# Banded attention scores and value products on quarters of TensorE's array, inside an attention and mixture-of-experts block

## The reference

```python
HEADS, HEAD_DIM, RADIUS = 16, 16, 7            # WIN = 15 keys around each query
qkv = xn @ qkv_w + qkv_b
scores = einsum('bld,blwd->blw', q, kw) / sqrt(HEAD_DIM)   # kw: the 15 keys around each token, zero padded
attn = softmax(scores, axis=-1)
out = einsum('blw,blwd->bld', attn, vw)                    # vw: the same window of the values
out = out @ proj_w + proj_b
```

## Time and profile before

| what | value |
|---|---|
| time, median of 3 runs | 2010.96 us (2010.38 to 2011.26) |
| time of the profiled execution | 2008.52 us |
| span of its instructions | 2006.8 us |
| PE busy in the span | 1978.0 us, 99% |
| PE weight loads busy | 1811.9 us, 90% |
| DVE busy | 1469.7 us, 73% |
| ACT busy | 1135.3 us, 57% |
| POOL busy | 923.8 us, 46% |
| granted TensorE clock, mean | 0.999 |

### The profile page before, as it was taken

One profiled execution on the slowest core, in us unless ns is written; L12 is line 12 of the kernel. 1 busy time (PEld: TensorE's weight loads), 2 busy tenths in 40 slices (PEclk: granted clock), 3 DMA queues, 4 the chain that ended last, 5 costly groups with the idle time before them and its releaser, 6 DMA issues.

```text
span 2006.8 us, 37534 instructions
## 1 busy us (share of the span) xinstructions
PE 1978.0 (99%) x13454; PEld 1811.9 (90%) x13454; DVE 1469.7 (73%) x2462; ACT 1135.3 (57%) x1801; POOL 923.8 (46%) x909
## 2 busy tenths in 40 slices
PE   7899999999999999999999999999999999999999
PEld 6789999999999999999999999999999999999998
DVE  8686786867868687786877868678686877868743
ACT  5465555646556555565655566465565555655554
POOL 6336254363434635255271553625446353453635
PEclk9999999999999999999999999999999999999999
DMA  4121211212112121121211102121021211212111
GB/s 122 32 64 53 54 53 32 70 49 69 49 32 64 43 74 44 48 58 32 74 53 53 48 27 74 53 61 52 29 72 43 74 43 46 55 38 74 43 58 53
DMA packets 188848, 108.79 MB, mean 54 GB/s; under 512 B 65436, under 2 KB 187640, under 8 KB 188664
## 3 DMA queue, kind: packets, MB, share of 16 engines
q1 hardware_dynamic: 187316, 105.43, 18.5%
q10 hardware_dynamic: 1348, 0.98, 0.2%
HBM read 85.52 MB, written 8.39 MB: 47 GB/s over the span
## 4 chain that ended last, share of the span: by engine, by line
PE 89%; DVE 6%; ACT 2%; issue 2%; SPq 0%; POOL 0%; DMA 0%; ACTq 0%; DVEq 0%; POOLq 0%
PE psB L233 48%; PE psA L233 25%; PE psA L1095 5%; PE psA L1122 5%; PE psA L1107 3%; PE psA L1010 2%; DVE pr L631 1%; DVE smax L627 1%; DVE hr_lo L553 1%; DVE qm L596 1%; DVE acc L569 1%; ACT hr_hi L860 0%; ACT pr L909 0%; ACT L909 0%; DVE rinv L629 0%
## 5 line engine op out<-in xcount | busy, mean ns | idle before, releaser
L553 DVE TENSOR_TENSOR hr_lo<-hf,hr_hi 128x512 fp32r<-128x512 f32 x512 | 485.7, 949 | 432.6 <-ACT hr_hi L860 431.9
L860 ACT ACTIVATE hr_hi<-hf 128x512 fp32r<-128x512 f32 x512 | 323.7, 632 | 272.8 <-PE psB L233 184.7
L440 POOL TENSOR_TENSOR wx_lo<-raw,wx_hi 128x512 fp32r<-128x512 f32 x256 | 393.4, 1537 | 21.4
L438 POOL TENSOR_SCALAR wx_hi<-raw 128x512 fp32r<-128x512 f32 x256 | 191.2, 747 | 363.6 <-PE psB L233 349.5
L856 ACT ACTIVATE hf<-psB,b1x 128x512 f32<-128x512 f32 x256 | 175.1, 684 | 199.4 <-PE psB L233 197.7
L233 PE MATMUL psB<-wx_hi,hr_hi 128*128 128x256 f32 x1024 | 287.5, 281 | 0.2
L233 PE MATMUL psB<-wx_hi,hr_lo 128*128 128x256 f32 x1024 | 286.3, 280 | 0.0
L233 PE MATMUL psB<-wx_lo,hr_hi 128*128 128x256 f32 x1024 | 285.7, 279 | 0.0
L454 POOL TENSOR_SCALAR kb<-kT 64x384 f32<-64x384 f32 x128 | 78.5, 613 | 351.3 <-ACT kT L876 343.4
L233 PE MATMUL psB<-z_hi,wx_hi 128*128 128x512 f32 x512 | 210.8, 412 | 0.0
L233 PE MATMUL psB<-z_hi,wx_lo 128*128 128x512 f32 x512 | 202.3, 395 | 0.0
(11 more groups left out here) (153 smaller groups left out, 5121.8 us busy)
## 6 DMA issues: line engine op xcount, KB each, us to landing
raw<-in_L_ffn_W1e SPq DMA_DIRECT2D x256, 128.0 KB, 2.2
raw<-in_L_ffn_W2e SPq DMA_DIRECT2D x256, 128.0 KB, 2.1
out_x<-acc SPq DMA_DIRECT2D x32, 256.0 KB, 2.2
xin<-in_L_attn_x SPq DMA_DIRECT2D x15, 512.0 KB, 3.8
vb<-vs SPq DMA_DIRECT2D x64, 96.0 KB
vb<-vs SPq DMA_DIRECT2D x62, 80.0 KB
tm<-in_L_ffn_b2e SPq DMA_DIRECT2D x32, 128.0 KB, 3.0
raw<-in_L_attn_fc_w SPq DMA_DIRECT2D x8, 256.0 KB, 4.0
```

What stands on the lines that cost most here:

```text
L438: g.tensor_scalar(wx[0][:, s, :], raw[:, s, :], 1.0, 0.0, ALU.mult, ALU.add).then_inc(w_hi.sem, 1)
L440: g.tensor_tensor(wx[1][:, s, :], raw[:, s, :], wx[0][:, s, :].bitcast(f32), ALU.subtract).then_inc(w_lo.sem, 1)
L553: v.tensor_tensor(hr[1][:, c % 2, :], hf[:, c % 3, :], hr[0][:, c % 2, :].bitcast(f32), ALU.subtract).then_inc(h_lo.sem, 1)
L860: a.activation(hr[0][:, c % 2, :], hf[:, c % 3, :], ACT.Copy).then_inc(h_hi.sem, 1)
```

## The change

1. **Scores** (scores): each block is now four products in place of one. Product (gr, n) takes features 64gr to 64gr+63 (a group of four heads) and two of the four copies of the queries: 64 rows by 64 columns of qm loaded, 64 by 48 of kT moving. The result goes to partitions 64n to 64n+63 of bank gr. All eight blocks of a unit fill both banks, 48 columns each, so one semaphore increment for each unit stands where there were two.
2. **No kb.** The windows are read in kT itself. POOL's copies (8 a row) go, and with them the semaphore kb; ACT's next write of kT, and DVE's of qm, now wait for score.
3. **Softmax layout.** pr is 128 by 16 by 64, of which 48 are used and 16 stay zero from a memset. mask h now reads bank h, which holds all blocks of one group, and writes with a gap.
4. **Transposes** have 112 columns in place of 96, and ACT's copies 112 partitions.
5. **attend**: each block is four products: 48 keys by 32 features (two heads) of vb loaded, 48 by 64 of pT (the same two heads) moving; the result goes to partitions 64gr + 32n of bank 2 + gr. vb has 64 features a row in place of 128 half empty.
6. **attended**: four operations as before, each on 64 partitions by 256, with emask (two heads) in place of hmask. POOL makes emask at the start, nine short operations more.

The core of the diff:

```diff
-    PK = G * KW
+    GW = 64
+    PK = GW + KW
+    HP = 32
...
-        kb = sb("kb", [P, 2, UB, G * KW])
...
-        vb = sb("vb", [PK, HS, NT, KD, P])
-        pr = sb("pr", [P, 2, UB, G, KW])
+        vb = sb("vb", [PK, HS, NT, KD, GW])
+        pr = sb("pr", [P, 2, UB, G, GW])
...
             def mask(t, u):
                 for h in range(2):
-                    v.wait_ge(score.sem, score.at(t, 2 * u + h))
+                    v.wait_ge(score.sem, score.at(t, u))
...
-                        pr[:, u % 2, 4 * h:4 * h + 4, :, :].rearrange("p b g k -> p (b g) k"),
-                        psA[:, h, 0:4 * G * KW].rearrange("p (n k) -> p n k", k=KW), HD ** -0.5,
-                        band[:, :].unsqueeze(1).to_broadcast([P, 4 * G, KW]), ALU.mult, ALU.add).then_inc(masked.sem, 1)
+                        pr[:, u % 2, :, h, 0:KW], psA[:, h, 0:UB * KW].rearrange("p (b k) -> p b k", k=KW), HD ** -0.5,
+                        band[:, :].unsqueeze(1).to_broadcast([P, UB, KW]), ALU.mult, ALU.add).then_inc(masked.sem, 1)
...
-                src = psA[:, 2:4, :].rearrange("p h (b s q) -> p (h b) s q", s=HS, q=QB)
-                dst = aT[:, c, th * UB * QB:(th + 1) * UB * QB].rearrange("p (b q) -> p b q", q=QB)
-                for s in range(HS):
-                    if s:
-                        v.wait_ge(aT_s.sem, aT_s.at(t, HS * u + s - 1))
-                        v.scalar_tensor_tensor(dst, src[:, :, s, :], hmask[:, s:s + 1], dst, ALU.mult, ALU.add).then_inc(aT_s.sem, 1)
-                    else:
-                        v.tensor_scalar(dst, src[:, :, s, :], hmask[:, s:s + 1], None, ALU.mult).then_inc(aT_s.sem, 1)
+                for n in range(2):
+                    for gr in range(G):
+                        rows = slice(GW * gr, GW * gr + GW)
+                        src = psA[rows, 2 + gr, :].rearrange("p (b n q) -> p b n q", n=2, q=QB)[:, :, n, :]
+                        dst = aT[rows, c, th * UB * QB:(th + 1) * UB * QB].rearrange("p (b q) -> p b q", q=QB)
+                        if n:
+                            v.wait_ge(aT_s.sem, aT_s.at(t, HS * u + gr))
+                            v.scalar_tensor_tensor(dst, src, emask[rows, n:n + 1], dst, ALU.mult, ALU.add).then_inc(aT_s.sem, 1)
+                        else:
+                            v.tensor_scalar(dst, src, emask[rows, n:n + 1], None, ALU.mult).then_inc(aT_s.sem, 1)
...
             def keys(t, c):
...
-                    a.wait_ge(kb_s.sem, kb_s.at(t, 3))
+                    a.wait_ge(score.sem, score.at(t, 1))
                 elif t:
-                    a.wait_ge(kb_s.sem, kb_s.all(t - 1))
+                    a.wait_ge(score.sem, score.all(t - 1))
...
             def scores(t, u):
...
-                    for j in range(4):
-                        b = 4 * h + j
-                        last = pe.matmul(psA[:, h, j * PK:(j + 1) * PK], qm[:, th, b, :], kb[:, th, b, :], start=True, stop=True)
-                    last.then_inc(score.sem, 1)
+                for b in range(UB):
+                    at = (th * UB + b) * QB
+                    for gr in range(G):
+                        rows = slice(GW * gr, GW * gr + GW)
+                        for n in range(2):
+                            cols = slice(2 * QB * n, 2 * QB * n + 2 * QB)
+                            last = pe.matmul(psA[cols, gr, b * KW:(b + 1) * KW], qm[rows, th, b, cols], kT[rows, at:at + KW], start=True, stop=True)
+                last.then_inc(score.sem, 1)
...
             def attend(t, u):
...
                     for j in range(4):
-                        last = pe.matmul(psA[:, 2 + h, j * P:(j + 1) * P], vb[:, j, 2 * th + h, c, :], pT[0:PK, 4 * h + j, :], start=True, stop=True)
+                        b = 4 * h + j
+                        for gr in range(G):
+                            keys = slice(GW * gr, GW * gr + KW)
+                            for n in range(2):
+                                to, cols = GW * gr + HP * n, slice(2 * QB * n, 2 * QB * n + 2 * QB)
+                                last = pe.matmul(psA[to:to + HP, 2 + gr, 2 * QB * b:2 * QB * (b + 1)], vb[keys, j, 2 * th + h, c, HP * n:HP * n + HP],
+                                                 pT[keys, b, cols], start=True, stop=True)
                     last.then_inc(av.sem, 1)
```

More of the change, by code:

```diff
@@ L109, in build @@
         hmask = sb("hmask", [P, HS])
+        emask = sb("emask", [P, 2])
         nb = sb("nb", [P, NT])
@@ L212, in build @@
         tr1, t1_f0, t1_f1, t1_hi, t1_lo = signal("tr1", KD), signal("t1_f0"), signal("t1_f1"), signal("t1_hi", KD), signal("t1_lo", KD)
[L213 removed]
+        qk, kT_s, qm_even, qm_odd = signal("qk", 4), signal("kT", KD), signal("qm_even", 8), signal("qm_odd", 8)
         val, vs_s, vb_in = signal("val", 2), signal("vs", 2), signal("vb_in", 12, 16)
[L215 removed]
+        score, masked, smax_s, shifted = signal("score", 4), signal("masked", 8), signal("smax", 4), signal("shifted", 4)
         exped, ssum, rinv_s = signal("exped", 4), signal("ssum", 4), signal("rinv", 4)
@@ L265, in windows @@
                 for gr in range(G):
-                    dst = vb[KW * gr + key:KW * gr + key + n, s, tiles[0]:tiles[-1] + 1, :, 64 * gr:64 * gr + 64]
+                    dst = vb[GW * gr + key:GW * gr + key + n, s, tiles[0]:tiles[-1] + 1, :, :]
                     src = vs[at:at + n, tiles[0] - back:tiles[-1] + 1 - back, :].rearrange("p i (c g n) -> p i c g n", c=KD, g=G)[:, :, :, gr, :]
@@ L407, in _ @@
             roots(1, *EXTRA[1])
[L408 to L412, removed]
+            for m, n in ((hmask, HS), (emask, 2)):
+                const(g.memset(m[:, :], 1.0))
+                for h in range(0, P, HD * n):
+                    v = m[h:h + HD * n, :]
+                    const(g.affine_select(out=v, in_=v, compare_op=ALU.is_ge, fill=0.0, base=0, pattern=[[-HD, n]], channel_multiplier=1))
+                    const(g.affine_select(out=v, in_=v, compare_op=ALU.is_ge, fill=0.0, base=HD - 1, pattern=[[HD, n]], channel_multiplier=-1))
             const(g.memset(band[:, :], 0.0))
@@ L440, in split @@
                 g.tensor_tensor(wx[1][:, s, :], raw[:, s, :], wx[0][:, s, :].bitcast(f32), ALU.subtract).then_inc(w_lo.sem, 1)
[L442 to L456, removed]
             def norm1_bias(t):
@@ L481, in _ @@
                         continue
[L482 to L487, removed]
+                    if q == 2 and t == 0:
+                        weights(8, 10)
+                        norm1_bias(0)
+                        weights(10, 13)
                     elif q == 7 and t:
@@ L590, in query_blocks @@
                 if c:
-                    v.wait_ge(score.sem, score.at(t, 2 * (u - 2) + 1))
+                    v.wait_ge(score.sem, score.at(t, u - 2))
                 elif t:
-                    v.wait_ge(score.sem, score.at(t - 1, 2 * (u + 2) + 1))
+                    v.wait_ge(score.sem, score.at(t - 1, u + 2))
                 src = psA[:, 3 if c or t == 0 else 1, th * UB * QB:(th + 1) * UB * QB].rearrange("p (b q) -> p b q", q=QB)
@@ L881, in query_blocks @@
                 if c:
-                    a.wait_ge(score.sem, score.at(t, 2 * (u - 2) + 1))
+                    a.wait_ge(score.sem, score.at(t, u - 2))
                 elif t:
-                    a.wait_ge(score.sem, score.at(t - 1, 2 * (u + 2) + 1))
+                    a.wait_ge(score.sem, score.at(t - 1, u + 2))
                 src = psA[:, 3 if c or t == 0 else 1, th * UB * QB:(th + 1) * UB * QB].rearrange("p (b q) -> p b q", q=QB)
@@ L899, in query_blocks_first @@
                 a.wait_ge(qk.sem, qk.at(t, 1))
-                a.wait_ge(score.sem, score.at(t - 1, 5))
+                a.wait_ge(score.sem, score.at(t - 1, 2))
                 src = psA[:, 1, 0:UB * QB].rearrange("p (b q) -> p b q", q=QB)
@@ L1078, in scores @@
                 pe.wait_ge((qm_odd if u % 2 else qm_even).sem, (qm_odd if u % 2 else qm_even).at(t, 4 * (u // 2) + 3))
-                pe.wait_ge(kb_s.sem, kb_s.at(t, 2 * u + 1))
-                for h in range(2):
-                    if u == 0 and t == 0:
-                        pe.wait_ge(kT_s.sem, kT_s.at(0, 0))
-                    elif u == 0 and h == 0:
-                        pe.wait_ge(vs_s.sem, vs_s.at(t, 0))
-                    elif u == 0:
-                        pe.wait_ge(qm_odd.sem, qm_odd.at(t, 3))
-                        if t > 1:
-                            pe.wait_ge(lg_s.sem, lg_s.at(t - 1))
-                    elif u == 1:
-                        pe.wait_ge(masked.sem, masked.at(t, h))
-                    else:
-                        pe.wait_ge(pT_s.sem, pT_s.at(t, 2 * (u - 2) + h))
-                    for j in range(4):
-                        b = 4 * h + j
-                        last = pe.matmul(psA[:, h, j * PK:(j + 1) * PK], qm[:, th, b, :], kb[:, th, b, :], start=True, stop=True)
-                    last.then_inc(score.sem, 1)
+                pe.wait_ge(kT_s.sem, kT_s.at(t, u // 2))
```

(13 more changed lines are left out.)

9 lines of the change are left out of this document (3 added, 6 removed).

## The result

The changed kernel takes 2016.1 us in the median of 17 runs (2011.5 to 2019.8), against 2011.6 us (2009.2 to 2015.1) before: 1.002 times, interval 1.0013 to 1.0028. It is slower by 0.2%, hardly more than can be told from no change. But inside it a good deal changed.

The account below looks back on a forecast made before the run. PE was taken to bound the kernel: 2008.5 + 218 (bursts) + 26 (switches) - 10 (waits) = 2242.5 us, or 2245 us as a median of runs. The wide range was 1925 to 2300 us, the forecast's own 2190 to 2300.

Parts of the forecast that it names:

- What bounds the kernel: Whole kernel: PE, busy 99% of the span, sets the time until DVE, busy 73%, binds.
- I take one at a time, because that is what all rows show: Scores and attend bursts: quarters work one after another, 53 ns a pass, 3.41 us a burst instead of 1.71: +218 us.
- The rule against small dimensions: Scores bursts: a matmul has some 60 cycles of overhead, so halving both sizes gains less, putting a burst above 3.41 us.
- Rival A: Scores and attend: all four quarters work at once, 0.85 us a burst, -110 us, 1935 us in all; chance 0.24.
- Switches, +26 us: Entering and leaving each burst: 256 switches between whole array and quarters at 0.1 us each; full drain would be 43 us.
- Waits of PE on DVE, -10 us: Before turns and scores: longer bursts give DVE time, so most of 11.8 us of PE's waits for softmax and qm goes.
- Keys: ... 0: POOL's queue: losing 128 key copies, 78.5 us, changes nothing, since no PE row waits for kb or expert splits: 0.
- B: Scores and attend: two quarters work at once, burst 1.71 us as now, plus switches: 2035 us; chance 0.10.
- C: Scores and attend: quarters work partly side by side, burst 2.0 to 3.0 us: 2130 us; chance 0.18.
- D: Scores and attend: a floor above 53 ns for each pass, whatever its size: 2315 to 2665 us; chance 0.06.
- Transposes, masks, attended: PE's transposes and DVE's mask and attended operations: loads stay under 128 moving columns, elements per partition unchanged: 0 each.

Follow-up runs that it names:

- e2: Changed kernel, with POOL waiting at step 2 until DVE has written the query blocks of the third unit: 1963.8 us, 0.9765 of the kernel before.
- e9: Kernel before the change, with a POOL wait for the third unit's query blocks added behind its second key copies: 2012.2 us, 1.0001.
- e4: Changed kernel, with the 32 products of a scores burst reordered: all eight blocks of one quarter, then the next: 2135.9 us (one run).
- e7: Changed kernel, with scores alternating between two quarters of the same columns and different rows, then the other two: 2030.2 us (one run).
- e8: Changed kernel, with scores alternating between two quarters of the same rows and different columns, then the other two: 2046.3 us (one run).
- e1: Changed kernel, with POOL waiting at step 2 until ACT has written kT for the second group of heads: 1970.6 us, 0.980 of the kernel before.
- e3: Kernel before the change, with POOL's copies of the second group's keys moved from step 2 to 4, behind two expert-weight splits: 2048.1 us, 1.018.

## Why the prediction was wrong

The forecast was 2245 us, slower by almost 12%. The measured 2016 us lies in the wide range and on the forecast's side, far below the forecast's own range of 2190 to 2300. That it came out slower at all is luck: two large errors with opposite signs met. The bursts took 83 us off PE (128 x 0.65) where 218 were to come on, and 79 us of waits and lost clock came where 10 were to go.

*What bounds the kernel:* right. PE was the bound, and of the 71 us of busy time that came off it 48 were won once the splits were held (e2 against e9). DVE was nearer to binding than the step had it.

*"I take one at a time, because that is what all rows show":* this step failed, and the +218 us with it. In the kernel before, every pass has a successor in the same array, so its rows could only show the pace of that case. e4 gives the pace for one quarter as 51 ns, where the step had worked out 53: the price of a column was right, the concurrency was not. The argument that two passes of one product share a quarter, so that a product overlaps its neighbour at best, did not hold either: that would give half of 3.28 us, and four in turn give 1.08 us a burst, three times faster than one at a time. The term was +218 us; measured, a burst is 0.62 to 0.68 us shorter, -83 us in 128 bursts.

*The rule against small dimensions* pointed the wrong way here. The Trainium skill ("TensorEngine Tiling (Array Packing)", Instruction Overhead) advises against cutting small ones, and the prediction put a burst above 3.41 us by it. 48 moving columns with loads of 64 cost 51 ns a pass in one quarter (e4), 3.28 us a burst, and 17 ns four abreast; no run shows what a pass costs when the load, too, is under 60 columns and stands alone. Its other rule, that tiles load and multiply in parallel (Key Properties), is what e4, e7 and e8 show.

*Rival A* had the mechanism, with 0.24. It gave 0.85 us a burst, measured 1.03 to 1.08; -110 us, measured -83 for the bursts and -71 of PE's busy time with the switches. It gave back 25 us for DVE becoming the bound; with the splits held that is about the size (71 less 48 is 23), in the changed kernel it was 79.

*Switches, +26 us:* too large. Entering costs 0.09 us more than before, near the 0.1 us taken, but leaving only 0.03, because most of its price was paid before as well: 128 x 0.12 = 15 us. The 43 us of a full drain at every entry did not come.

*Waits of PE on DVE, -10 us:* the wrong sign, +66.5 us in the whole span, which follows from the burst step and the next one. It also counted too much to win: the 3.6 us for qm are PEld's and the 1.7 us PE's record of the same bursts.

*"Keys: ... 0":* the second step that failed. It asked whether PE waits for kb or for splits, found that it does not, and priced the removal at nothing. It should have asked what the waiting copy held back and where that would go: 10 us earlier, beside DVE's critical stretch. The row that POOL waited 343 us for kT was the warning. The term was 0; measured, the splits set free cost 46 to 52 us (e1 and e2 against the changed kernel).

*The other rivals:* B (two at once) and C (partly) are what e7 and e8 had to force by their order; D, a floor for each pass above 53 ns, is ruled out by 16 to 17 ns a pass, and so is its burst of 4.0 us.

*Transposes, masks, attended:* as said. The mask takes 549 ns in place of 548 and DVE waited 0.2 us for scores; the four operations of attended take 481 to 483 ns; eight transposes take 0.84 us in place of 0.83.

## What to carry to other kernels

Float32 products that fill a quarter of the array gained here from standing next to products in other quarters, in rows or columns alike (3.28 us a burst became 1.08); issued one quarter after the other they only cost (3.28 us where whole-array products took 1.70). Before removing work from an engine that is not the bottleneck, look for what is queued behind its waits: a copy that waits can be what keeps its queue off a shared resource, and a bare wait can take its place. When a change on the bottleneck moves nothing, compare the mean times of unchanged operations on the other engines first.

## What the runs showed of the hardware

- 64 float32 passes on quarters: 3.28 us in one quarter, 1.81 in two rows, 1.82 in two columns, 1.08 in four. A burst of whole-array products (16 passes) takes 1.70.
- Going from whole-array passes to quarters took 0.09 us more than going to whole-array float32 passes did, and coming back 0.03 us more.
- DVE's two-input operation on 128 by 1024 takes 1.22 us alone and 2.21 beside a POOL split; a reduction of 128 by 768 takes 0.94 in both cases.
- Waits of PE of 1.15 and 1.70 us in one row were followed by a granted clock of 0.50, and like waits in other rows were not. In e3, where PE's instructions are unchanged, the mean granted clock is 0.993 instead of 0.999 and PE's busy time 14.3 us longer.
